# Last attention by pairs of batches, and the last feed-forward layer with gates first and eight banks

## What is computed

```python
# last attention: q is layernorm(x); k and v are the context; pe: position codes
ngb = einsum('bqd,bkd->bqk', q + pe[pos], k + pe[pos])
grp = einsum('bqd,bkd->bqk', q + pe[pos // 16 + 60], k + pe[pos // 16])
attn = where(mask, where(causal, ngb, -inf), where(causal, grp, -inf))
x = x + softmax(attn) @ v
# last feed-forward; act_qdq rounds by the largest absolute value of the WHOLE tensor
x1 = act_qdq(layernorm(x))
up, gate = act_qdq(x1 @ deq(w_up).T), act_qdq(x1 @ deq(w_gate).T)
gate = act_qdq(gate * round_u16(sigmoid(gate)))
x = x + act_qdq(gate * up) @ deq(w_down).T
```

## Time and profile before

| | us |
|---|---|
| median of 3 runs | 1546.83 (1544.35 to 1546.91) |
| the profiled execution, its own time | 1546.87 |
| span of that execution in the profile | 1545.1 |
| of it after the expert loop's end, about 1360 | 185.1 |

### The profile page before, as it was taken

How to read it: one execution, slowest core, us unless ns; L and a number is a source line. 1 busy time by engine, 2 the same in 40 slices (tenths; PEclk the granted TensorE clock), 3 DMA queues, 4 the chain that set the end, 5 groups by cost and what they waited for, 6 DMA issues and landing times.

```text
span 1545.1 us, 29908 instructions
## 1 busy us (share of the span) xinstructions
PE 1302.3 (84%) x9616; PEld 932.9 (60%) x9616; DVE 987.3 (64%) x2308; ACT 726.6 (47%) x2096; POOL 499.0 (32%) x544
## 2 busy tenths in 40 slices
PE   4888789999979999979988999889969799966603
PEld 3676677777755666557776777656645566644203
DVE  2766366676766555666775666656677845568696
ACT  3666156565634444447775777522212233321542
POOL 6500266666625000052213222120040057732070
PEclk9999699999999999999999999979988799965856
DMA  7000000000005555510000000012210066501000
GB/s 260 8 8 19 1 1 1 0 0 0 1 1 165 187 190 191 186 48 2 0 0 2 1 0 0 2 47 85 85 58 1 1 169 165 146 23 32 0 0 27
DMA packets 40086, 81.68 MB, mean 53 GB/s; under 512 B 5411, under 2 KB 22851, under 8 KB 39893
## 3 DMA queue, kind: packets, MB, share of 16 engines
q1 hardware_dynamic: 40020, 80.84, 16.7%
HBM read 79.18 MB, written 1.64 MB: 52 GB/s over the span
## 4 chain that ended last, share of the span: by engine, by line
PE 61%; DVE 14%; ACT 14%; issue 7%; POOL 2%; DMA 1%; ACTq 0%; DVEq 0%; SPq 0%; POOLq 0%
PE score_bank L1414 15%; ACT h_all L939 10%; PE f_bank L1443 7%; PE f_bank L1178 5%; PE score_bank L1259 5%; PE turn_bank L1275 4%; PE out_bank L1443 3%; PE turn_bank L1443 3%; PE out_bank L1315 3%; PE out_bank L1284 2%; PE score_bank L1250 2%; PE f_bank L1571 1%; PE out_bank L1324 1%; DVE work L1658 1%; PE f_bank L1199 1%
## 5 line engine op out<-in xcount | busy, mean ns | idle before, releaser
L1414 PE MATMUL score_bank<-parts 128*128 128x512 f32 x1040 | 396.2, 504 | 8.6 <-DVE parts L1792 7.1
L939 ACT ACTIVATE h_all<-score_bank,top_score 128x128 f32<-128x128 f32 x896 | 281.6, 401 | 114.7 <-DVE top_score L1646 114.6
L1414 PEld LDWEIGHTS score_bank<-parts 128*128 128x128 f32 x1040 | 202.2, 195 | 161.0 <-issue 115.0
L1646 DVE TENSOR_REDUCE top_score<-score_bank 128x4 f32<-128x512 f32 x224 | 142.9, 680 | 136.8 <-PE score_bank L1259 136.8
L1443 PE MATMUL f_bank<-h_all,wset 128*128 128x512 f32 x260 | 136.6, 607 | 14.7 <-DVE h_all L1889 12.9
L1877 DVE TENSOR_TENSOR h_all<-work,h_all 128x512 f32<-128x512 f32 x124 | 91.2, 738 | 85.8 <-ACT h_all L1043 85.7
L1043 ACT ACTIVATE h_all<-score_bank,wset 128x512 f32<-128x512 f32 x128 | 87.8, 687 | 116.1 <-PE score_bank L1414 116.0
L1275 PE MATMUL turn_bank<-CF,h_all 128*128 128x128 f32 x512 | 83.4, 286 | 42.7 <-DVE work L1658 23.2
L702 POOL TENSOR_TENSOR small<-small,half_neg 128x4 f32<-128x4 f32 (+2 forms) x22 | 36.3, 1655 | 241.3 <-DVE small L1619 128.6
L1275 PEld LDWEIGHTS turn_bank<-CF,h_all 128*128 128x128 f32 x512 | 56.3, 144 | 69.1 <-ACT h_all L939 22.7
L1039 ACT ACTIVATE rope_c<-score_bank 128x512 f32<-128x512 f32 x66 | 39.4, 597 | 112.6 <-PE score_bank L1414 99.4
(11 more groups left out here) (360 smaller groups left out, 2748.4 us busy)
## 6 DMA issues: line engine op xcount, KB each, us to landing
work<-gates_l0m SPq DMA_DIRECT2D x62, 512.0 KB, 3.7
W0X<-gates_l2m SPq DMA_DIRECT2D x32, 256.0 KB, 3.8
CTX<-gates_l2m SPq DMA_DIRECT2D x32, 256.0 KB, 3.8
wset<-in_l0m SPq DMA_DIRECT2D x32, 128.5 KB, 3.4
W0X<-gates_l1m SPq DMA_DIRECT2D x8, 512.0 KB, 3.6
wset<-in_l1m SPq DMA_DIRECT2D x8, 384.0 KB, 3.1
CTX<-gates_l1m SPq DMA_DIRECT2D x6, 512.0 KB, 3.7
cT<-in_ctxT SPq DMA_DIRECT2D x32, 64.0 KB, 1.8
```

The costliest lines, as they stand in the source:

```text
L939: last = act.activation(held[c][:, P * m:P * m + P], score_bank[c][:, P * m:P * m + P], ACT.Exp, bias=top_score[c][:, m:m + 1], **sums)
L1414: last = pe_.matmul(bk[:, :], wt[s % 2][:, col:col + P], y[:, x], start=(part == 0), stop=(part == len(parts_of) - 1))
L1646: dve.tensor_reduce(top_score[c][:, :], split(score_bank[c][:, :], HEADS), AX_X, ALU.max, negate=True)\
```

## The change

The keys and values of all batches are loaded by three large DMAs before the l2m gates are known (into `work` and `AO`), and VectorE adds the position codes to the keys in eight instructions (`place_keys`) in the first two steps of the l2m loop. The adds to X leave the last step of that loop and follow it. The attention goes by pairs of batches over five groups of banks. ScalarE normalises (scale and bias by column); TensorE transposes four batches at a time; one VectorE instruction makes the queries of four batches. Scores of both kinds of a pair fill one bank; one VectorE instruction takes the negated maximum of each row over both kinds; ScalarE takes the exponential from PSUM with that as bias and sums the row. TensorE joins the kinds: it multiplies both halves of the exponentials by the identity into the same columns. The masked kind gives zero. `stream` is a row of bf16 products whose result isn't used.

In the last feed-forward ScalarE normalises, the gate part's 12 products come before the up part's 12, eight banks hold them, one VectorE maximum covers three banks' worth, and the scaling of the up part by its step is left out (the factor goes into the next scale); the subtraction of the rounding constant moves from GpSimd to ScalarE (`other`). The last products go by quarters of the tokens. The removed code is what the section before describes; the added core, with the indentation cut:

```diff
+keys3 = work[:, 0:4096].rearrange("p (b m t) -> p b m t", m=2, t=P)
+queries3 = [work[:, 1024 * t + 4096:1024 * t + 5120].rearrange("p (b m t) -> p b m t", m=2, t=P) for t in range(2)]
+probs3, turned3 = hT[0:2], [t[:, 0:2 * P] for t in hT[2:4]]
+front3, scores3, turn3, out3 = f_bank[0], score_bank[0:3], v_bank, [f_bank[1], score_bank[3]]
+tokens4 = [front3, score_bank[2], score_bank[0], score_bank[1]]
+ring8 = turn3 + out3 + tokens4
...
+def keys_and_values():
+    r, k = front_use("turn_w3", 3)
+    sp.wait_ge(f_drained[r], k + 1)
+    for m in range(2):
+        load(keys3[:, :, m, :], a["ctxT"].rearrange("b p n -> p b n"), in_keys)
+    load(AO[:, :, :], a["ctx"].rearrange("b s d -> s b d"), in_keys)
...
+if name in ("l3x", "l3m"):
+    link(last)
+    link(pool.tensor_tensor(less_mean[:, lo:hi], mean[:, lo:hi], r1[:, lo:hi], ALU.mult))
+    last = pool.tensor_scalar(shift[:, lo:hi], less_mean[:, lo:hi], -1.0, None, ALU.mult)
...
+def normalise(n, g):
+    part = next(p for p, (_, hi) in enumerate(PARTS[n]) if hi >= 4 * g + 4)
+    act.wait_ge(rooted, part_at[n] + part + 1)
+    for b in range(4 * g, 4 * g + 4):
+        last = act.activation(Y[:, b, :], X[:, b, :], ACT.Identity, scale=r1[:, b:b + 1], bias=shift[:, b:b + 1])
+    last.then_inc(step(n + ".y"), 1)
+def exponentials3(j):
+    act.wait_ge(maxed3, j + 1)
+    if j >= 2:
+        act.wait_ge(turned3_made, j - 1)
+    for x in range(2):
+        b, cols = 2 * j + x, slice(2 * P * x, 2 * P * x + 2 * P)
+        last = act.activation(probs3[j % 2][:, cols], scores3[j % 3][:, cols], ACT.Exp, bias=top3[:, b:b + 1],
+                              accum_out=sum3[:, b:b + 1])
+    last.then_inc(exped3, 1)
+def copy3(j):
+    act.wait_ge(turned3_made, j + 1)
+    if j >= 2:
+        act.wait_ge(weighed3, j - 1)
+    act.activation(turned3[j % 2], turn3[j % 2][:, 0:2 * P], ACT.Copy).then_inc(copied3, 1)
+normalise("l3x", 0)
+normalise("l3x", 1)
+exponentials3(0)
+normalise("l3x", 2)
+exponentials3(1)
+copy3(0)
+normalise("l3x", 3)
+for j in range(2, PAIRS):
+    exponentials3(j)
+    copy3(j - 1)
+copy3(PAIRS - 1)
+for g in range(4):
+    normalise("l3m", g)
...
+def copies(w, c):
+    for m in range(3):
+        e = 12 * (1 - w) + 3 * c + m
+        act.wait_ge(products_made, e + 1)
+        act.activation((U3, G3)[w][:, m, BANK * c:BANK * c + BANK], ring8[e % 8][:, :], ACT.Copy)\
+            .then_inc(products_copied, 1)
...
+def other(at):
+    act.wait_ge(step("l3m.u_round"), at + 1)
+    act.activation(piece(U, at), piece(U, at), ACT.Identity, bias=less_magic[:, :]).then_inc(step("l3m.u"), 1)
+for c in range(4):
+    copies(1, c)
+copies(0, 0)
+act.wait_ge(step("l3m.scale"), 2)
+for at in range(6):
+    rounded(big, at, 2, "l3m.g_round")
+    if at < 3:
+        copies(0, at + 1)
+    if at == 4:
+        act.wait_ge(step("l3m.scale"), 3)
+    if at >= 4:
+        rounded(U, at - 4, 1, "l3m.u_round")
+    sigmoid(at)
+for at in range(2, 6):
+    rounded(U, at, 1, "l3m.u_round")
+for at in range(4):
+    other(at)
 act.wait_ge(step("l3m.scale"), 4)
+for at in range(6):
+    rounded(big, at, 3, "l3m.round3")
+    if 1 <= at <= 2:
+        other(at + 3)
 act.wait_ge(step("l3m.scale"), 5)
+for q in (1, 2):
+    part = G3[:, :, BANK * q:BANK * q + BANK]
+    act.activation(part, part, ACT.Identity, scale=quant[:, 4, 3:4], bias=magic).then_inc(step("l3m.round4"), 1)
...
+def fronts3(g):
+    pe_.wait_ge(step("l3x.y"), g + 1)
+    if g:
+        pe_.wait_ge(queried3, g)
+    for m in range(4):
+        last = pe_.transpose(front3[:, P * m:P * m + P], Y[:, 4 * g + m, :], ident)
+    last.then_inc(fronted3, 1)
+def score3(j):
+    pe_.wait_ge(queried3, j // 2 + 1)
+    pe_.wait_ge(placed3, j + 1)
+    if j >= 3:
+        pe_.wait_ge(exped3, j - 2)
+    bk = scores3[j % 3]
+    pe_.matmul(bk[:, :], ident_bf, own_bf.unsqueeze(1).to_broadcast([P, 2, 2 * P]), start=True, stop=False, skip_group_check=True)
+    for x in range(2):
+        b = 2 * j + x
+        for m in range(2):
+            cols = slice(2 * P * x + P * m, 2 * P * x + P * m + P)
+            last = pe_.matmul(bk[:, cols], queries3[j // 2 % 2][:, b % 4, m, :], keys3[:, b, m, :],
+                              start=False, stop=True, skip_group_check=True)
+    last.then_inc(scored3, 1)
+def turn_probs3(j):
+    bk = turn3[j % 2]
+    if j < 2:
+        pe_.wait_ge(x_added, 2 * CHUNKS + 3 + j)
+    else:
+        pe_.wait_ge(copied3, j - 1)
+    stream(2, bk)
+    pe_.wait_ge(exped3, j + 1)
+    for x in range(2):
+        for m in range(2):
+            last = pe_.matmul(bk[:, P * x:P * x + P], probs3[j % 2][:, 2 * P * x + P * m:2 * P * x + P * m + P], ident,
+                              start=(m == 0), stop=(m == 1))
+    last.then_inc(turned3_made, 1)
+def weigh3(j):
+    pe_.wait_ge(copied3, j + 1)
+    if j >= 2:
+        pe_.wait_ge(added3, 2 * j - 2)
+    for x in range(2):
+        last = pe_.matmul(out3[j % 2][:, P * x:P * x + P], turned3[j % 2][:, P * x:P * x + P], AO[:, 2 * j + x, :],
+                          start=True, stop=True)
+    last.then_inc(weighed3, 1)
+def tokens_of(g):
+    pe_.wait_ge(step("l3m.y"), g + 1)
+    if g:
+        pe_.wait_ge(exped3, {1: 6, 2: 7, 3: 8}[g])
+    else:
+        pe_.wait_ge(queried3, 4)
+    for m in range(4):
+        last = pe_.transpose(tokens4[g][:, P * m:P * m + P], Y[:, 4 * g + m, :], ident)
+    last.then_inc(tokens_turned, 1)
+pe_.wait_ge(in_keys, 16 * 3)
+fronts3(0)
+score3(0)
+fronts3(1)
+score3(1)
+turn_probs3(0)
+for j in range(2, PAIRS):
+    score3(j)
+    weigh3(j - 2)
+    turn_probs3(j - 1)
+    if j in (2, 4):
+        fronts3(j // 2 + 1)
+weigh3(PAIRS - 2)
+turn_probs3(PAIRS - 1)
+weigh3(PAIRS - 1)
 for g in range(4):
+    tokens_of(g)
+    if g == 2:
+        stream(8, turn3[0])
+stream(12, turn3[0])
+for e in range(24):
+    w, c, m = 1 - e // 12, e % 12 // 3, e % 3
+    if w:
+        pe_.wait_ge(tokens_scaled, c + 1)
+    if e >= 8:
+        pe_.wait_ge(products_copied, e - 7)
+    elif e >= 4:
+        pe_.wait_ge(tokens_rounded, e - 3)
+    elif e >= 2:
+        pe_.wait_ge(added3, B)
+    at = 3 * (1 - w) + m
+    pe_.matmul(ring8[e % 8][:, :], W3T[:, P * at:P * at + P], YT[:, BANK * c:BANK * c + BANK], start=True, stop=True)\
+        .then_inc(products_made, 1)
...
+pe_.wait_ge(products_copied, 24)
+pe_.wait_ge(step("l3m.p"), 5)
+stream(16, ring8[4])
+for q in range(4):
+    pe_.wait_ge(hidden_ready, q + 1)
...
+    if n == "l2m" and isinstance(i, int) and i == 0:
+        place_keys(CHUNKS * s + c)
...
+def place_keys(t):
+    dve.wait_ge(in_keys, 16 * 3)
+    r, k = front_use("turn_w3", 0)
+    dve.wait_ge(f_drained[r], k + 1)
+    two = keys3[:, 2 * t:2 * t + 2]
+    places = PET[:, :].rearrange("p (m s) -> p m s", m=3)[:, 0::2, :].unsqueeze(1).to_broadcast([P, 2, 2, P])
+    dve.tensor_tensor(two, two, places, ALU.add).then_inc(placed3, 1)
...
+def queries3_of(g):
+    dve.wait_ge(fronted3, g + 1)
+    if g >= 2:
+        dve.wait_ge(scored3, 2 * g - 2)
+    src = split(front3[:, :], 4).unsqueeze(2).to_broadcast([P, 4, 2, P])
+    places = split(PET[:, 0:2 * P], 2).unsqueeze(1).to_broadcast([P, 4, 2, P])
+    dve.tensor_tensor(queries3[g % 2], src, places, ALU.add).then_inc(queried3, 1)
+def largest3(j):
+    dve.wait_ge(scored3, j + 1)
+    dve.tensor_reduce(top3[:, 2 * j:2 * j + 2], split(scores3[j % 3][:, :], 2), AX_X, ALU.max, negate=True)\
+        .then_inc(maxed3, 1)
+def add3(j):
+    dve.wait_ge(exped3, j + 1)
+    two = slice(2 * j, 2 * j + 2)
+    link(dve.reciprocal(rec3[:, two], sum3[:, two]))
+    dve.wait_ge(weighed3, j + 1)
+    for x in range(2):
+        b = 2 * j + x
+        dve.scalar_tensor_tensor(X[:, b, :], out3[j % 2][:, P * x:P * x + P], rec3[:, b:b + 1], X[:, b, :],
+                                 ALU.mult, ALU.add).then_inc(added3, 1)
+    for x in range(2):
+        dve.wait_ge(added3, 2 * j + x + 1)
+        measure(X, 2 * j + x)
+add(0)
+measured(0)
+add(1)
+measured(1)
+queries3_of(0)
+add(2)
+largest3(0)
+measured(2)
+largest3(1)
+add(3)
+queries3_of(1)
+measured(3)
+for j in range(2, PAIRS):
+    largest3(j)
+    if j in (3, 5):
+        queries3_of(j // 2 + 1)
+    add3(j - 2)
+variances("l3m", 0)
+add3(PAIRS - 2)
+add3(PAIRS - 1)
+variances("l3m", 1)
...
+def chunk_max(w, c):
+    dve.wait_ge(products_copied, 12 * (1 - w) + 3 * c + 3)
+    at = 12 * w + 3 * c
+    return largest(part_max[:, at:at + 3], (U3, G3)[w][:, :, BANK * c:BANK * c + BANK])
...
+for c in range(4):
+    last = chunk_max(1, c)
+join_max(last, 2, slice(12, 24))
+chunk_max(0, 0)
+scale(2, 2)
 gate_steps(0)
+chunk_max(0, 1)
+gate_steps(1)
+chunk_max(0, 2)
+last = chunk_max(0, 3)
+join_max(last, 1, slice(0, 12))
+for at in range(6):
+    last = by_sigmoid(at)
+    if at == 0:
+        scale(1, 3)
+    if at < 4:
+        gate_steps(at + 2)
+join_max(last, 3, slice(0, 6))
...
+def round_quarter(q):
+    link(dve.tensor_scalar(quarter(q), quarter(q), quant[:, 4, 3:4], MAGIC, ALU.mult, ALU.add))
+def scale_quarter(q):
```

(9 more changed lines are left out.)

336 lines of the change are left out of this document (88 added, 248 removed).

## The result

| | us |
|---|---|
| before, median beside the changed kernel (4 executions) | 1546.87 (1544.35 to 1551.95) |
| after, median of 4 executions | 1495.81 (1494.25 to 1498.74) |
| ratio, with its 95% interval | 0.9668 (0.9640 to 0.9697) |
| after, the profiled execution: its time, its span | 1494.25, 1492.5 |

The columns are those of the earlier trace rows.

A forecast was written before the change was run, and what follows sets the result against it. It took five serial stages behind the expert loop as the bound, with no engine full in the last attention. Gains and losses summed to 43.6 us, less 3 allowance: 1545.1 to 1504.5 of span, 1506 us in all; range 1497 to 1520.

The forecast's parts named there:

- Key placing: Eight VectorE additions in the last expert loop, four beside GpSimd's gate multiplications; a loss of 1.5 us.
- Rival B: In the last expert loop, key placing waits for whole gate multiplications and holds the loop: +5 us, 1511; chance 0.15.
- The adds leaving the last step: At the end of the last expert loop, its last multiplication can begin about 1.2 us earlier.
- Loads: Three 1 MB loads issued some 70 us before VectorE wants them, taking 22 us: hidden.
- Rival C: Loads arrive late and VectorE stands at place_keys from 1235: 1524 us, or 1550 if slower; chance 0.05.
- The attention: From the adds behind the loop to the last add to X: pairs 3.3 us each at full clock; gain 26.2 us.
- rival A: In the last attention the clock stays at 1.2 GHz, pairs take 6.3 us instead of 3.3: +18, 1524; chance 0.12.
- To the first product: From the attention's last add to X to the first feed-forward product: 9.2 us against 12.0, gain 2.8.
- Products: From the first product to the gate scale: 15.6 us against 25.8, gain 10.2.
- Gate steps: From the gate scale to the third scale, VectorE without GpSimd beside it: 37.8 us against 43.6, gain 5.8.
- The allowance: 3 us set against the summed gain for hand-offs that such a sum leaves out.
- Rival D: The clock never falls and is full from the attention's first pair: -5 us, no allowance needed, 1498; chance 0.15.

The follow-up runs named there:

- keys_unadorned: The changed kernel without the eight additions that place the keys, their waits kept; median 1501.7 us.
- subtraction_on_gpsimd: The changed kernel with the six subtractions of the up half moved from ScalarE back to GpSimd, without the scaling pass after each; median 1510.2 us.
- two_banks: The changed kernel with gate and up products waiting for the copy two before them instead of eight before; median 1505.5 us.

## Why the prediction came out as it did

- **The ground of the sum.** "My sum goes along the span's clock": I took everything before 1235 from one profiled execution, as unchanged, and gave it no width. This is the step that failed, with 10.6 of the 12.0 us. The same code reaches the last multiplication anywhere between 1350 and 1361. 2.6 of the 10.6 us are the luck of the profiled execution (the ten of the changed kernel have their last multiplication at 1352.7 on average), and 1.6 are that of the one before (1360.33, where the average is 1358.8). 1.7 are GpSimd's shorter start, which I put at nothing, 1.4 to 2.3 the next two terms, and 2.3 to 3.2 stay open in these ten executions. Had the range carried the scatter, 4 us either way, it would have held the result, by its width and not by a right sum: the average of the ten, 1496.8, lies 9 us below the forecast.
- **Slips in the sum.** The terms from the loop to the first scores add up to 1369.9 and not 1370.4, 1378 + 5 x 3.3 is 1394.5 and not 1394.8, and those to the first product are 7.9 us and not 8.2. The first is swallowed by the "about 1378" behind it; the other two made the forecast 0.6 us too long.
- **Key placing**, 1.5 us forecast: 0.3 by keys_unadorned. Rival B is out. Three of the eight additions do wait for the rest of a GpSimd pass, 1.6 us in all, but in time that VectorE has.
- **The adds leaving the last step**: priced as 1.2 us gained in the loop, where it gives 1.4 to 2.3, it costs 1.4 to 3.2 in all. I looked at what left the loop and not at VectorE, which is what the start of the attention waits for.
- **Loads**: hidden. They landed 8.3 and 11.3 us after issue, and no wait for them shows. Rival C is out.
- **The attention**, 40.7 forecast, 40.9 measured: scores of pair 0 after 10.9 us (10.6 forecast), of pair 2 after 18.0 (18.2), pairs 3.3 apart (3.3). The choice of 2.4 GHz was right (0.92 over the stretch, 1.00 from 1370), rival A is out, and not because of the stream products: without them the clock is full from 1380 on. No run takes the other parts of the attention's change (pairs, early loads, the joining on TensorE) back one by one.
- **To the first product**, 9.2 forecast, 12.1 measured: the mis-sized term. The 12 normalisations that were to "lie under the chain" stand behind the last copy in ScalarE's queue, and behind GpSimd's power. The all-reduce, taken at 0.5 us, begins 5.8 us after GpSimd's last power, a row that the trace of before showed, covered.
- **Products**, 15.6 and 15.7. Two banks cost 0.9 us here and 4.4 in the gate steps, so 9.2 us of the gain don't need the eight banks. No run puts the old order of the products back; that it is the order stays argued.
- **Gate steps**, 37.8 and 36.2; **last scales**, 19.6 and 19.6, with ScalarE late by 2.0 for the foreseen 2.3; **the end**, 17.3 and 17.2.
- **The allowance** of 3 us was used up by the first product. Rival D's mechanism, a clock full from the start, didn't happen (0.92 over the attention, 0.72 to the first product); its 1498 was near for other reasons.

## What to carry to other kernels

Before a stage-by-stage sum, ask how far the untouched part moves from execution to execution, put that width into the range, and judge small edits by the length from a fixed instruction to the end and not by a median of four, and look into several traces before a difference below 1 us is read. When a cover goes, look at what ended just behind it: the row that will bound the stage next is often already there. Two edits that each win little may win more together.

## What the runs showed of the hardware beyond this

- The granted clock of unchanged code differs between executions: 95 to 133 us at 1.2 GHz ahead of the tail, a scatter of 4.1 us in 1545.
- A turn of GpSimd from ordinary instructions to an all-reduce: 5.80 to 6.23 us in each of 16 cases whose input came earlier than that; between two all-reduces with nothing ordinary in between, the second began 0.1 us behind its input. The turn back: 6.94, 6.97 and 7.06 us.
- Products that only warm the array do not always keep the clock, and the length of the idleness behind them doesn't say when: with 1.84 and 1.96 us of it the first quarter of the final products ran at 1.2 GHz (subtraction_on_gpsimd, two_banks), with 2.03 to 2.81 us in five other kernels it ran at 2.4.
